# One attention and expert layer on one core: the main scores follow the maximum scores by one pipeline step in place of two

## The chip, the core and the metric

The kernel runs on one core of a Trainium2 chip, as one launch. The core's engines are named here as in the profile: PE is TensorE (matmuls), DVE is VectorE, ACT is ScalarE, POOL is GpSimd, SP is SyncE, which issues most of the DMAs. The metric is the device time of one execution in microseconds, and smaller is better. Before the change three runs gave a median of 390.14 us, from 389.27 to 390.70.

## The reference

The input is x, 32 sequences of 128 rows of 128 numbers, and ctx of the same shape. The layer computes, cut to what matters:

```
q = layernorm(x);  k = v = ctx                       # 16 heads of 8
energy = einsum('nqhd,nkhd->nhqk', q, k)
attn = softmax(energy / sqrt(128));  out = attn @ v
x = x + tanh(g_xattn) * (out @ w_out.T + b_out)
logits = layernorm(x) @ Wg                           # 8 experts
two best experts for each row; weights = softmax of the logits over the two
each row is sent to its two experts: gelu(row @ W1[e] + b1[e]) @ W2[e] + b2[e]
x = x + tanh(g_ffn) * (weighted sum of the two answers)
```

## The kernel before, in words

It has two large parts. The first does attention, the second layer norm, the choice of experts and the scattering of rows into an expert-ordered table in DRAM, one sequence of 128 rows after the other. The second part (71 tiles of 128 gathered rows, each through the two matrices of its expert) starts when the last row is scattered and a table of tiles has been computed from the counts. A last short part adds the two answers of each row and stores the result.

The first part is a software pipeline written out by hand. `pipeline(step)` (line 271) calls `step` once for each t from -2 to 41, so 44 steps, on each engine with that engine's own `step`. A step gets twelve stage names, each of them the sequence that this stage handles in this step, t plus the stage's offset, or None where there is none. The offsets stand in one line (269). In this order:

- n (t+2), x (t+1): statistics of the first layer norm, and the normalised row `xn`.
- a (t): PE transposes `xn` and ctx (lines 622, 623), ACT copies them to `kT` and `qT` (525, 527), and PE computes the first half of the maximum scores (`max_scores(a, 0)`, line 598). These are bf16 scores that serve only to find each row's maximum.
- m (t-1): PE computes the second half of the maximum scores, and DVE reduces both halves to `negmax` (`maximum(0)` and `maximum(1)`, line 779, 1.2 us each).
- b (t-3): PE transposes `negmax` (line 605), ACT copies it to `mT` (510), PE computes the main scores in f32 (630) and subtracts the maxima by a matmul with `pick` (635), and ACT takes the exponential (534). POOL adds the bias to x (442) and copies the values (454).
- p (t-4): probabilities times values (671), and ACT's copy of them (539). q (t-5): transposes and normalisation (652, 813, 820). c (t-6): output projection, x updated, statistics (608, 645, 816, 826). w, r, k (t-7, t-8, t-9): second layer norm, logits, choice, places. d (t-10): POOL scatters the sequence's rows by two indirect DMAs (line 427).

The engines meet at semaphores. Each engine runs its instructions in the order of its step function: on PE the transposes of b, c, r, then those of a, then the main scores of b, then the second half of m's maximum scores, then the small matmuls of c, r, q, k, then 671, and last the first half of a's maximum scores. Both halves of the maximum scores write the same two PSUM banks, so each waits for the reduction of the half before it: `max_scores(s, h)` waits for 2s+h reductions. `negmax` has three buffers, `kT` and `qT` have four, and the main scores' banks wait for the exponentials of the sequence before.

At t = 0 POOL writes its constants, at t = 1 PE transposes the output weights (580, 581) and at t = 2 DVE scales them. PE starts step 2 only when that is done, and POOL's first b waits for it too. SP loads x and ctx in six chunks at the start, and from then on issues one side transfer (expert weights, zeros) for each a.

Of the kernel before, what the change touches and what calls it, by code (L numbers as in the profile page):

```python
# [36 lines left out]
def flamingo_layer(nc, x, ctx, g_xattn, g_ffn, w_out, b_out, Wg, W1, b1, W2, b2, out):  # L37
# [29 lines left out]
    with ExitStack() as es:  # L67
# [198 lines left out]

            return CHUNKS.index(s) if s in CHUNKS[:-1] else None

        N_AT, X_AT, A_AT, M_AT, B_AT, P_AT, Q_AT, C_AT, W_AT, R_AT, K_AT, D_AT = 2, 1, 0, -1, -3, -4, -5, -6, -7, -8, -9, -10

        def pipeline(step):

# [677 lines left out]
```

How the kernel before makes its waits and increments, by code:

```python
        def wait(eng, semaphore, value):  # L248
            if isinstance(value, int) and value < 1:
                return
            eng.wait_ge(semaphore, value)
# [1 line left out]
        def wait_alone(eng, semaphore, value):  # L254
            eng.wait_ge(const_done, 1)
            eng.wait_ge(semaphore, value)
# [23 lines left out]
        def write_pads(eng, experts):  # L282
            eng.wait_ge(pad_tab_done, 1)
            ends = [eng.value_load(pad_tab[0:1, e:e + 1], min_val=0, max_val=PAD_ROW) for e in experts]
            for u in range(NX):
                eng.wait_ge(row_out[u], 32 * (B // NX))
            for r in ends:
                eng.dma_start(xs_dram[bass.ds(r, P), :], pad[:, :]).then_inc(pads_out, 16)
# [22 lines left out]
        @block.sync  # L312
# [30 lines left out]
                pair = slice(k // 2 * 2, k // 2 * 2 + 2)  # L343
                if k < E and k % 2 == 0:
                    sp.dma_start(ex_sb[:, pair, 0:FF], w1v[:, pair, :]).then_inc(moe_loaded, 16)
                elif k < E:
                    sp.dma_start(w2s[:, pair], w2v[:, pair]).then_inc(moe_loaded, 16)
                elif k == E:
                    sp.dma_start(ex_sb[:, :, FF:FF + D], b2.partition_broadcast(P)).then_inc(moe_loaded, 16)
                elif k <= E + NZ:
                    sp.dma_start(zrows[k - E - 1], zeros[:, :]).then_inc(zeroed, 16)
            sp.wait_ge(pool_const, 1)
            def step(t, n, x, a, m, b, p, q, c, w, r, k, d):
                if a is not None and a >= 2:
                    sp.wait_ge(qkT_ready, a)
                    side_transfer(a - 2)
```

## Time and profile before

| what | us |
|---|---|
| median of three runs | 390.14 |
| the profiled execution | 391.28 |
| its span | 389.0 |
| PE, DVE busy in the span | 307.3, 274.0 |
| ACT, POOL busy in the span | 222.6, 223.2 |
| first part, until POOL's last scatter has been issued | 205.17 |
| first matmul of the expert part | 215.27 |

The profile is of one execution. What lies around the span is the difference between 391.28 and 389.0, which is 2.28 us. The steps of the pipeline can be found on PE: from t = 3 to t = 34 a step starts with line 605, once for each sequence of stage b, 32 times. A timeline row gives the start, the length, the engine and line, the operation with its tiles, how many instructions of this kind were run together (x8), and in brackets how long the engine had been idle before it and what released it.

### The profile page before, as it was taken

To read this page: it belongs to the slowest core of one execution; us is meant where nothing else is said; L and a number is where in the kernel's file an instruction comes from. 1 tells how busy PE (TensorE), PEld (TensorE's weight loads), DVE (VectorE), ACT (ScalarE), POOL (GpSimd) and SP (SyncE) were. 2 spreads that over 40 slices of the span, in tenths; PEclk is the share of its full clock that TensorE was granted. 3 is DMA by queue.
4 is the path that set the end of the run, shared out by engine and by line. 5 is a ranking of instruction groups with operands and counts; after the bars stand their busy time and mean duration, and the time that the engine had idled before them with its cause. 6 is when DMAs were issued, how large, how long until landed. Compare 5 with 4: busy or idle time off the path is not lost.

```text
span 389.0 us, 13777 instructions
## 1 busy us (share of the span) xinstructions
PE 307.3 (79%) x3993; PEld 251.1 (65%) x3994; DVE 274.0 (70%) x1084; ACT 222.6 (57%) x656; POOL 223.2 (57%) x367
## 2 busy tenths in 40 slices
PE   1688988989999999987510899999999999999100
PEld 0345665656666566665410899999999998999100
DVE  3858999999999999995673355555555554555296
ACT  2368887777788777765101355555555555555140
POOL 2522457877777877777770155555555555555262
PEclk9999999999999999999955699999999999999655
DMA  7953332122222110100112122222222222221396
GB/s 197 299 168 110 110 98 76 57 79 83 85 78 83 56 52 29 37 31 30 37 48 70 48 69 68 60 63 67 61 64 67 62 64 57 65 61 42 99 358 192
DMA packets 40157, 33.85 MB, mean 87 GB/s; under 512 B 4998, under 2 KB 32936, under 8 KB 40112
## 3 DMA queue, kind: packets, MB, share of 16 engines
q1 hardware_dynamic: 35216, 24.58, 21.6%
q0 software_dynamic: 4320, 8.43, 6.8%
q8 instruction: 25, 0.41, 0.5%
q10 hardware_dynamic: 576, 0.26, 0.3%
q14 instruction: 20, 0.16, 0.2%
HBM read 17.95 MB, written 15.77 MB: 87 GB/s over the span
## 4 chain that ended last, share of the span: by engine, by line
PE 36%; DMA 5%; DVE 4%; POOL 3%; issue 3%; SPq 1%; DVEq 0%; POOLq 0%
PE main_scores L697 17%; PE main_scores L711 17%; POOL expert_rows L427 3%; PE max_scores L688 2%; DVE x_all L920 2%; DVE x_all L924 2%; DMA yc<-choice_rows 1%; DMA choice_rows<-y_s,dest 1%; DMA expert_rows<-pad 1%; DMA expert_rows<-xrow,slot_i 1%; DMA xt<-expert_rows 1%; SPq L289 0%; SPq L390 0%; DVE y_s L901 0%; POOL choice_rows L481 0%
## 5 line engine op out<-in xcount | busy, mean ns | idle before, releaser
L481 POOL DMA_INDIRECT choice_rows<-y_s,dest x71 | 78.8, 1110 | 80.0 <-DVE y_s L901 66.2
L552 ACT ACTIVATE hT<-main_scores,ex_cur 128x128 f32<-128x128 f32 x284 | 81.0, 368 | 68.9 <-PE main_scores L697 68.9
L779 DVE TENSOR_REDUCE negmax<-max_scores 128x8 bf16<-128x1024 f32 x64 | 77.7, 1213 | 6.4 <-PE max_scores L598 6.2
L427 POOL DMA_INDIRECT expert_rows<-xrow,slot_i x64 | 64.8, 1012 | 26.9 <-PE mixed L648 14.1
L711 PE MATMUL main_scores<-w_sb,hT 128*128 x568 | 78.9, 282 | 0.3 <-ACT hT L552 0.3
L697 PE MATMUL main_scores<-xtT,ex_cur 128*128 128x128 f32 x568 | 78.2, 282 | 0.8 <-DVE xtT L893 0.8
L697 PEld LDWEIGHTS main_scores<-xtT,ex_cur 128*128 128x128 f32 x568 | 70.6, 195 | 2.1 <-DVE xtT L893 1.0
L891 DVE COPY ex_cur<-ex_sb 128x644 f32 x71 | 35.2, 496 | 49.7 <-ACT hT L552 25.6
L711 PEld LDWEIGHTS main_scores<-w_sb,hT 128*128 128x128 f32 x568 | 68.9, 191 | 1.6 <-issue 0.5
L534 ACT ACTIVATE probs<-main_scores 128x1024 f32<-128x1024 f32 x64 | 62.0, 1021 | 8.4 <-issue 4.9
L630 PE MATMUL main_scores<-qT,kT 32*128 32x512 f32 x256 | 38.4, 669 | 4.0 <-ACT mT L510 3.9
L527 ACT ACTIVATE qT<-mixed,head_mask 128x128 f32<-128x128 f32 x128 | 37.0, 386 | 0.0
L598 PE MATMUL max_scores<-kT,qT 32*128 32x128 bf16 x512 | 27.5, 226 | 11.8 <-DVE negmax L779 6.5
L671 PE MATMUL mixed<-probs,values 128*32 128x128 f32 x1024 | 35.4, 280 | 0.0
L688 PE MATMUL max_scores<-ident,xt 128*128 128x128 f32 x71 | 20.6, 290 | 16.5 <-DMA xt<-expert_rows 16.5
L598 PEld LDWEIGHTS max_scores<-kT,qT 32*128 32x128 bf16 x512 | 17.5, 97 | 22.8 <-issue 14.9
L458 POOL TENSOR_TENSOR rstd<-ve,neg_half 128x1 f32<-128x1 f32 x32 | 17.9, 560 | 24.6 <-DVE ve L764 24.6
L901 DVE TENSOR_TENSOR y_s<-main_scores,ex_cur 128x128 f32<-128x128 f32 x71 | 20.7, 291 | 15.8 <-PE main_scores L711 13.4
L671 PEld LDWEIGHTS mixed<-probs,values 128*32 128x32 f32 x1024 | 26.6, 111 | 1.6 <-issue 0.9
L465 POOL TENSOR_TENSOR rstd<-ve,neg_half 128x1 f32<-128x1 f32 x32 | 17.7, 553 | 13.7 <-DVE ve L764 13.2
L893 DVE COPY xtT<-max_scores 128x128 f32<-128x128 f32 x71 | 20.1, 284 | 7.4 <-PE max_scores L688 7.4
L635 PEld LDWEIGHTS main_scores<-mT,pick 32*128 32x128 bf16 x512 | 12.1, 96 | 17.7 <-issue 17.7
(132 smaller groups left out, 472.8 us busy)
## 6 DMA issues: line engine op xcount, KB each, us to landing
xt<-expert_rows SPq DMA_DIRECT2D x71, 64.5 KB, 1.8
choice_rows<-zeros SPq DMA_DIRECT2D x16, 256.0 KB, 2.3
yc<-choice_rows SPq DMA_DIRECT2D x16, 256.0 KB, 5.9
ex_sb<-in_L_ffn_W_dram SPq DMA_DIRECT2D x4, 512.0 KB, 4.9
w_sb<-in_L_ffn_W_dram SPq DMA_DIRECT2D x4, 512.0 KB, 4.6
out_dram<-x_all SPq DMA_DIRECT2D x8, 256.0 KB, 4.2
x_all<-in_x_dram SPq DMA_DIRECT2D x5, 384.0 KB, 6.0
ctx_all<-in_ctx_dram SPq DMA_DIRECT2D x5, 384.0 KB, 6.3
```

The source lines that it names most:

```text
L427: nc.gpsimd.indirect_dma_start(xs_dram, bass.IndirectOffsetOnAxis(ap=slot_i[:, d % NX, i:i + 1], axis=0), xrow[:, d % NX, i, :], None).the ...
L481: nc.gpsimd.indirect_dma_start(y_dram, bass.IndirectOffsetOnAxis(ap=dest[:, v, :], axis=0), y_s[:, v, :], None, bounds_check=last_row, oob ...
L527: last = nc.scalar.activation(qT[:, a % KQ, j, :], QK_T[:, 0:P], ACT.Copy, scale=head_mask[:, j:j + 1])
L534: nc.scalar.activation(probs[:, b % 2, 2 * g:2 * g + 2, :].rearrange("p g k -> p (g k)"), E_ALL[:, 1024 * g:1024 * g + 1024], ACT.Exp, sca ...
L552: last = nc.scalar.activation(hT[:, v % 2, c, :], H_BANK[v % 2][:, c * P:c * P + P], ACT.Gelu, bias=ex_cur[:, v, FF + D + c:FF + D + c + 1])
L598: last = nc.tensor.matmul(S_BANK[g % 2][:, j * P:j * P + P], qT_high[strip, s % KQ, j, :], kT_high[strip, s % KQ, :], start=True, stop=True)
L630: nc.tensor.matmul(E_BANK[g], kT[strip, b % KQ, :], qT[strip, b % KQ, :, :].rearrange("p j q -> p (j q)"), start=True, stop=False, skip_gr ...
L671: last = nc.tensor.matmul(O_ALL[32 * g:32 * g + 32, h2 * P:h2 * P + P], values[:, p % 2, h2, j, g, :], probs[:, p % 2, g, head:head + P], ...
L697: last = nc.tensor.matmul(H_BANK[v % 2][:, c * P:c * P + P], ex_cur[:, v, c * P:c * P + P], xtT[:, v % 2, :], start=True, stop=True)
L711: last = nc.tensor.matmul(Y_BANK[v % 2][:, 0:D], hT[:, v % 2, c, :], w2_sb[:, bass.ds(e * (NF * D) + c * D, D)], start=(c == 0), stop=(c = ...
L779: V.tensor_reduce(negmax[:, m % 3, 2 * h:2 * h + 2, 0:J], S_ALL[:, :].rearrange("p (g j k) -> p g j k", g=2, j=J), AX.X, ALU.max, negate=T ...
L891: V.tensor_copy(ex_cur[:, v, :], ex_sb[:, bass.ds(e, 1), :].rearrange("p e f -> p (e f)")).then_inc(ex_ready, 1)
```

## The change

Ten stage offsets move by one. n, x, a and m stay, and b and all behind it come one step sooner. So b takes the sequence whose maxima were reduced in the step directly before, where it took the one of two steps before. The distance between b and each stage behind it stays as it was. The last t is B - D_AT - 1, so the pipeline has 43 steps.

```diff
-        N_AT, X_AT, A_AT, M_AT, B_AT, P_AT, Q_AT, C_AT, W_AT, R_AT, K_AT, D_AT = 2, 1, 0, -1, -3, -4, -5, -6, -7, -8, -9, -10
+        N_AT, X_AT, A_AT, M_AT, B_AT, P_AT, Q_AT, C_AT, W_AT, R_AT, K_AT, D_AT = 2, 1, 0, -1, -2, -3, -4, -5, -6, -7, -8, -9
```

On PE, at the start, the instructions from line 598 of step 1 on stand in a row like this before; the row 598 x16 joins the second half of one step and the first half of the same step's next sequence:

```order
L598 MATMUL max_scores<-kT,qT 128x128 x16
L622 MATMUL mixed<-ident,xn 128x128
L623 MATMUL mixed<-ident,ctx_all 128x128
L598 MATMUL max_scores<-kT,qT 128x128 x16
L605 MATMUL mixed<-ident_b,negmax 128x128
L622 MATMUL mixed<-ident,xn 128x128
L623 MATMUL mixed<-ident,ctx_all 128x128
L630 MATMUL main_scores<-qT,kT 128x512 x4
```

And like this in the changed kernel:

```order
L598 MATMUL max_scores<-kT,qT 128x128 x16
L605 MATMUL mixed<-ident_b,negmax 128x128
L622 MATMUL mixed<-ident,xn 128x128
L623 MATMUL mixed<-ident,ctx_all 128x128
L630 MATMUL main_scores<-qT,kT 128x512 x4
L635 MATMUL main_scores<-mT,pick 128x128 x16
L598 MATMUL max_scores<-kT,qT 128x128 x16
```

The step that held only 622, 623 and 598 (step 2) now holds the transposed maxima and the main scores of the first sequence too.

On PE, near the end of the pipeline, the rows behind the last row 598 (the second half of the last sequence's maximum scores, step 32) are these before, cut at the first row of step 34's kind; line 605 here starts step 33:

```order
L605 MATMUL mixed<-ident_b,negmax 128x128
L608 MATMUL mixed<-ident,attn 128x128
L611 MATMUL mixed<-ident,xrow 128x128
L630 MATMUL main_scores<-qT,kT 128x512 x4
L635 MATMUL main_scores<-mT,pick 128x128 x16
L645 MATMUL mixed<-woutT,aT 128x128
```

In the changed kernel the 31st line 605 is still in a step with maximum scores:

```order
L605 MATMUL mixed<-ident_b,negmax 128x128
L608 MATMUL mixed<-ident,attn 128x128
L611 MATMUL mixed<-ident,xrow 128x128
L630 MATMUL main_scores<-qT,kT 128x512 x4
L635 MATMUL main_scores<-mT,pick 128x128 x16
L598 MATMUL max_scores<-kT,qT 128x128 x8
L645 MATMUL mixed<-woutT,aT 128x128
```

What moved: before, two steps (33 and 34) compute main scores with no maximum scores beside them, and afterwards one step (33) does.

## Rows read from the trace of the kernel before

**Rows 1.** The page: span, busy shares, and TensorE's granted clock in 40 slices.

```profile
span 389.0 us, 13777 instructions
...
PE 307.3 (79%) x3993; PEld 251.1 (65%) x3994; DVE 274.0 (70%) x1084; ACT 222.6 (57%) x656; POOL 223.2 (57%) x367
...
PEclk9999999999999999999955699999999999999655
```

**Rows 2.** Windows view: length, busy time (instructions) of each engine, clock, DMA.

```profile
core 0: us, PE busy (x) PEld busy (x) DVE busy (x) ACT busy (x) POOL busy (x), PEclk, DMA share, GB/s
64.00:159.08 95.08, 87.60 (x1566) 59.10 (x1567) 92.73 (x397) 74.56 (x198) 74.54 (x145) 1.00 0.19 66
169.36:174.39 5.03, 3.96 (x78) 2.86 (x78) 4.74 (x19) 2.91 (x6) 3.59 (x7) 1.00 0.10 30
174.39:179.18 4.79, 3.72 (x69) 2.62 (x70) 2.52 (x19) 2.87 (x6) 3.60 (x7) 1.00 0.10 29
179.18:184.20 5.02, 3.73 (x70) 2.64 (x70) 2.57 (x19) 2.81 (x6) 3.75 (x8) 1.00 0.12 39
```

**Rows 3.** Timeline of PE, fill: start, length, line, operation, [idle before].

```profile
14.09 0.47 PE L622 MATMUL mixed<-ident,xn 128*128 128x128 f32 x1
...
18.05 0.29 PE L605 MATMUL mixed<-ident_b,negmax 128*128 128x128 bf16 x1
...
18.69 2.09 PE L630 MATMUL main_scores<-qT,kT 32*128 32x512 f32 x8
...
21.00 0.64 PE L598 MATMUL max_scores<-kT,qT 32*128 32x128 bf16 x8
...
23.59 0.29 PE L605 MATMUL mixed<-ident_b,negmax 128*128 128x128 bf16 x1
...
27.19 1.88 PE L671 MATMUL mixed<-probs,values 128*32 128x128 f32 x32
29.01 0.40 PE L598 MATMUL max_scores<-kT,qT 32*128 32x128 bf16 x8
29.58 0.23 PE L605 MATMUL mixed<-ident_b,negmax 128*128 128x128 bf16 x1 [0.17 <-ACT oS L539]
...
33.96 0.23 PE L605 MATMUL mixed<-ident_b,negmax 128*128 128x128 bf16 x1 [0.29 <-ACT oS L539]
```

**Rows 4.** Timeline of DVE, fill: the last reduction of step 1, the first of step 2.

```profile
12.07 1.21 DVE L779 TENSOR_REDUCE negmax<-max_scores 128x8 bf16<-128x1024 f32 x1
...
14.07 1.22 DVE L779 TENSOR_REDUCE negmax<-max_scores 128x8 bf16<-128x1024 f32 x1
```

**Rows 5.** Timeline of PE, full steps: first and last start of line 605.

```profile
63.99 0.23 PE L605 MATMUL mixed<-ident_b,negmax 128*128 128x128 bf16 x1
...
164.34 0.23 PE L605 MATMUL mixed<-ident_b,negmax 128*128 128x128 bf16 x1 [0.16 <-ACT oS L539]
```

**Rows 6.** Timeline of PE, drain: the first matmuls of steps 33, 34 and 35.

```profile
174.39 0.23 PE L605 MATMUL mixed<-ident_b,negmax 128*128 128x128 bf16 x1 [0.49 <-ACT oS L539]
...
179.18 0.23 PE L605 MATMUL mixed<-ident_b,negmax 128*128 128x128 bf16 x1 [0.49 <-ACT oS L539]
...
184.20 0.33 PE L608 MATMUL mixed<-ident,attn 128*128 128x128 f32 x1 [0.71 <-ACT oS L539]
```

**Rows 7.** Timeline of POOL, drain: first and last of the last 14 scatters.

```profile
185.47 1.05 POOL L427 DMA_INDIRECT expert_rows<-xrow,slot_i  x1 [0.86 <-PE mixed L611]
...
204.22 0.95 POOL L427 DMA_INDIRECT expert_rows<-xrow,slot_i  x1 [0.30 <-issue]
```

**Rows 8.** Timelines of DVE and PE, one full step: second reduction, and line 605 behind it.

```profile
104.70 1.21 DVE L779 TENSOR_REDUCE negmax<-max_scores 128x8 bf16<-128x1024 f32 x1
...
106.60 0.23 PE L605 MATMUL mixed<-ident_b,negmax 128*128 128x128 bf16 x1
```

**Rows 9.** Windows view, behind the drain: the expert part's first matmuls, and the clock.

```profile
218.00:220.00 2.00, 2.00 (x11) 2.00 (x10) 0.35 (x2) 1.14 (x4) 0.00 (x0) 0.50 0.26 63
220.00:222.00 2.00, 2.00 (x20) 2.00 (x20) 0.50 (x2) 1.14 (x4) 0.00 (x0) 0.99 0.13 33
```

## The prediction, as it was made before the changed kernel ran

> **What bounds the kernel now.** I read the page first, then the busy times of stretches, then the timelines of PE and DVE at both ends of the pipeline. The page [rows 1] says that PE is busy 79% of the span and DVE 70%, which names no bound, because the parts differ. The windows [rows 2] do. In the stretch from 64.0 to 159.08 us, when every stage is at work, DVE is busy 92.73 of 95.08 us (98%), PE 87.60, ACT 74.56, POOL 74.54. So in a full step DVE sets the pace, with PE close behind. Such a step lasts (164.34 - 63.99) / 19 = 5.28 us [rows 5]: the two starts of line 605 are those of steps 12 and 31.
>
> At the ends it is otherwise. In steps 33 and 34, which start at 174.39 and 179.18 [rows 6], DVE is busy only 2.52 of 4.79 and 2.57 of 5.02 us [rows 2]. There the chain PE, ACT, PE, DVE within a step is the bound. In the fill, step 2 (14.09 to 18.05) has only front stages, and steps 3 and 4 (18.05 to 23.59, 23.59 to 29.58) have the main scores too [rows 3].
>
> Both ends lie on the path that sets the end: the expert part waits for the last scatter. POOL issues the last 14 scatters from 185.47 to 204.22 [rows 7], and the tables, the pad rows and the first gather stand behind them.
>
> **The sum.** No instruction is added or taken away in number. What changes is which stages share a step. Call a step's front its n, x, a, m and its back the rest. Before, step t holds front t and the back that begins with sequence t-3; now it begins with t-2. So one step with a front alone goes (old step 2), one step with a back alone goes (old step 33), and the two halves so freed are one more full step. Step by step:
>
> 1. Steps 0 and 1 are the same to the instruction, and end at 14.09 as before.
>
> 2. New step 2 does what old step 3 did: line 605, the transposes, the main scores at 2.09 us for eight, line 635, both halves of the maximum scores and a reduction between them [rows 3]. It needs the maxima of sequence 0. The reduction that ends them runs from 12.07 for 1.21 us [rows 4], so it is over at 13.29, before the step starts. Old step 3 took 23.59 - 18.05 = 5.54 us. New step 2 then ends at 14.09 + 5.54 = 19.63, and new step 3 starts with what old step 4 started with at 23.59. Gain: 3.96 us, exactly old step 2. The first reduction of step 2 (14.07 to 15.29 [rows 4]) lies beside the main scores.
>
> 3. From there new step t does what old step t+1 did, up to the end of the fronts. A step's fronts come later in time than before (front 3 at 19.6 where it was 18.05), so no chunk of x or ctx can be late that wasn't, and SP's side transfers move by the same 1.5 us or so to the later side; the expert weights are not wanted before 215 us.
>
> 4. The fronts end with step 31 in both. So new steps 3 to 31 are old steps 4 to 31 and one full step more: minus 5.28 us.
>
> 5. New step 32 is like old step 32 (5.03 us). Step 33 is like old step 34. Old step 33 is gone: plus 4.79 us.
>
> 6. From old step 35 on (184.20 [rows 6], POOL's scatter at 185.47) everything is as it was, one step number sooner: the same 14 scatters, tables, pads. This tail moves with what is ahead of it.
>
> Sum: 3.96 + 4.79 - 5.28 = 3.47 us less. The profiled execution of 391.28 us (span 389.0 and 2.28 around it) would be 387.81, its span 385.5. It was 1.14 us above the median, so the median becomes 390.14 - 3.47 = 386.67.
>
> **The wait that is made shorter.** Line 605 of sequence s now reads `negmax` that DVE wrote in the step before. By the code this costs nothing at any step: line 605 in step t+1 asks for 2(t-1)+2 = 2t reductions, and the first half of a's maximum scores, the last thing that PE did in step t, has asked for 2t as well. PE never reaches line 605 without them. The trace shows the same distance in a full step [rows 8]: the second reduction ends at 104.70 + 1.21 = 105.91 and line 605 starts at 106.60, 0.69 us later. Queued behind it on PE is the whole step, and ACT's `mT`, so this would be dear if it were wrong. In the fill, 13.29 against 14.09, the slack is 0.8. Below nothing it can't go either, since these waits were no wait before. I take 0; the upper end is the rival below. The buffers get looser: `kT`, `qT` and `negmax` are free one step sooner, and no row shows that anything waits for them, so I take 0 for that too, at most the 2.35 us (95.08 - 92.73) by which DVE is idle in 18 full steps [rows 2], since DVE can't gain more than that.
>
> **The clock.** Step 2's matmuls, and those of steps 3 and 4, run at half speed: eight of line 598 take 0.64 us at 21.00 and 0.40 from 29.01 on [rows 3]. The granted clock in the page [rows 1] reads near full in these slices, so it doesn't show this early stretch; the row lengths do. PE went to full speed between 27.19 and 29.01, that is 8.5 to 10.3 us after the first main scores (18.69), the first dense work. My sum assumes that the rise moves with the work, and so comes near 24.5. The same holds at the start of the expert part, where the granted clock is 0.50 until 220 and 0.99 behind it [rows 9], some 4.7 us after that part's first matmul (215.27 in the table of times). If either rise is half a step off, the half-speed stretch is some 2 us longer or shorter, and half of that is time: 1 us either way.
>
> The Trainium skill, "TensorE: Matmul & The Clock Gate", part 1 (the clock gate), says that the half rate is the default, that sustained activity releases it, and that the point of release differs from run to run, because the watch doesn't start with the kernel. By this rule the rise need not follow the work by the same distance, which would be the second rival below; the rows before show one rise in the fill only, so this trace can neither confirm nor deny it.
>
> **Rivals.**
>
> The forecast, 386.7 us, own range 385.4 to 388.1: chance 0.68.
>
> The clock rises where it did, at some 28.4 us, though the work is earlier. Then new step 3 is slow to its end and takes some 6.4 in place of 5.99 us, so it ends at 26.0, and the 2.4 us that follow are done at half speed: they hold what takes about 2.4 x 4.38 / 6.4 = 1.6 us at full speed (4.38 is old step 5, 29.58 to 33.96 [rows 3]). Loss 0.4 + 0.8 = 1.2 us, so 387.9. For it speaks that 9 us of dense work had to pass before; against it, that the dense work itself begins 4 us sooner. Chance 0.11, half of it beyond the 0.5% line.
>
> It gains more: the earlier dense work, now with main scores directly behind the first maximum scores, raises the clock a step sooner than the shift. Old step 4 (5.99) would be near old step 5 (4.38): 1.6 us more, 385.1. Chance 0.05.
>
> No change: POOL, not the chain, holds the drain. In old step 33 POOL is busy 3.60 of 4.79 us [rows 2]. If POOL were behind there, dropping the step would give back only its idle time, 4.79 - 3.60 = 1.19, and the sum is 3.96 + 1.19 - 5.28 = -0.13: 390.3. For it speaks that the last scatters run one behind the other; against it, that POOL is idle in a quarter of each of the steps before, so it enters the tail with no backlog. Chance 0.08.
>
> Slower: line 605 does wait for the reduction in every full step, so the chain reduction, 605, `mT`, main scores, maximum scores, reduction closes into a ring longer than 5.28 us. It decides as soon as the wait is over 3.47 / 29 = 0.12 us in each of 29 steps. At most it is a reduction less today's distance, 1.21 - 0.69 = 0.52 us; at 0.3 it would cost 29 x 0.3 = 8.7, less 3.5: 395.3. For it: DVE is the bound and the ring goes through it. Against it: the equal counts above. Chance 0.05.
>
> The change does only half of what it says: the fill gains, but the full step that comes back is longer than it looks or the drained steps are not shorter, so that the net is under 1 us: 389.6. Chance 0.03.
>
> **How the numbers follow.** The predicted time is the forecast's, 386.7 us. Its bounds are the clock's 1 us either way and 0.3 us of scatter. Left out of 385.0 to 389.0 are the no-change, slower and half-gain cases (0.16) and a thin tail below, 0.2 in all at most. 0.5% is 1.95 us, about what a measurement can tell here, so faster means below 388.2: 0.66 of the forecast, 0.06 of the clock rival, and 0.05 of the larger gain, together 0.77, and with the share of the half-gain cases that fall there 0.8. Within 0.5%: the rest of the clock case, the POOL case and the half gain, 0.15. Slower 0.05.
>
> **What would show it.** PE's line 605 first at about 14.1 and 19.6 us, 32 times; full steps of 5.28 us; the last matmul of line 598 near 173 us, 1.3 us later than before, but line 605's last start near 175.7 in place of 179.18; POOL's last scatter near 200.8; the first matmul of the expert part near 211.8, and the expert part as long as it was. Wrong for the ring: idle time before line 605 put down to DVE's `negmax`, and full steps over 5.4 us. Wrong for the clock: eight of line 598 at 0.61 us beyond 25 us. Wrong for POOL: the scatters at the usual place, near 204, though PE has finished early.

## The result: 2.2 us faster where 3.5 were forecast

On the chip of the first measurement the kernel before took 390.69 us (median of 20 runs, 389.27 to 392.43) and the changed kernel 388.77 us (20 runs, 387.05 to 389.57). The ratio is 0.9944, with a 95% interval from 0.9932 to 0.9956, so 2.2 us faster, from 1.7 to 2.7 (the two medians lie 1.9 us apart). The forecast was 3.47 us (386.7 us, from 390.14), range 385.0 to 389.0. The time lies in that range and the direction is right. It lies above 385.4 to 388.1, the narrower range of the forecast's own case, and of the 2.1 us between 386.7 and 388.77 some 0.55 are the base, which measured 390.69 in place of 390.14. The gain is 0.6 of what was forecast.

The page of the changed kernel, the lines that answer to [rows 1]:

```profile
span 386.6 us, 13778 instructions
...
PE 307.7 (80%) x3993; PEld 251.2 (65%) x3994; DVE 274.2 (71%) x1084; ACT 222.6 (58%) x656; POOL 222.6 (58%) x367
...
PEclk9999999999999999999655799999999999999655
```

The same work is done in 2.4 us less of span in this pair of traces. The starts of the steps on PE, which answer to [rows 3] and [rows 6], are in its timeline (start, length, engine, line, operation, idle before it):

```profile
13.81 0.29 PE L605 MATMUL mixed<-ident_b,negmax 128*128 128x128 bf16 x1
...
14.50 2.09 PE L630 MATMUL main_scores<-qT,kT 32*128 32x512 f32 x8
...
19.40 0.29 PE L605 MATMUL mixed<-ident_b,negmax 128*128 128x128 bf16 x1
...
23.00 1.22 PE L671 MATMUL mixed<-probs,values 128*32 128x128 f32 x32
...
24.99 0.23 PE L605 MATMUL mixed<-ident_b,negmax 128*128 128x128 bf16 x1
...
170.96 0.23 PE L605 MATMUL mixed<-ident_b,negmax 128*128 128x128 bf16 x1 [0.16 <-ACT oS L539]
...
175.99 0.23 PE L605 MATMUL mixed<-ident_b,negmax 128*128 128x128 bf16 x1 [0.49 <-ACT oS L539]
...
181.00 0.33 PE L608 MATMUL mixed<-ident,attn 128*128 128x128 f32 x1 [0.71 <-ACT oS L539]
...
212.12 0.91 PE L688 MATMUL max_scores<-ident,xt 128*128 128x128 f32 x2 [16.36 <-DMA xt<-expert_rows]
```

The main scores of the first sequence start at 14.50, inside step 2, and steps 2, 3 and 4 start at 13.81, 19.40 and 24.99. No line 605 waits for `negmax`. The 32 matmuls of line 671 at 23.00 take 1.22 us, where those at 27.19 took 1.88 in the kernel before, so PE comes to full speed about 4 us earlier than it did: the rise came with the work. In the drain, step 32 starts at 170.96, step 33 at 175.99, and what was step 35 starts at 181.00 in place of 184.20.

The tail moved as a block: the last 14 scatters on POOL answer to [rows 7].

```profile
182.27 1.05 POOL L427 DMA_INDIRECT expert_rows<-xrow,slot_i  x1 [0.85 <-PE mixed L611]
...
201.04 0.96 POOL L427 DMA_INDIRECT expert_rows<-xrow,slot_i  x1 [0.30 <-issue]
```

From the first of them to the last it is 18.77 us, and 18.75 before. In this pair of traces the pipeline ends 204.22 - 201.04 = 3.18 us sooner, near the 3.47 of the forecast, while the spans differ by 2.4 and the 20 runs say 2.2. So the question is what a typical pair gives, and which term is too large.

**Which term.** The steps from the first full-speed one to the end of the fronts are 27 before (steps 5 to 31) and 28 after (steps 4 to 31). Their length in the windows view, the kernel before first (columns as in [rows 2]):

```profile
29.58:169.36 139.78, 127.64 (x2321) 86.78 (x2322) 134.55 (x544) 110.91 (x293) 98.50 (x199) 1.00 0.22 73
```

And the changed kernel:

```profile
24.99:170.96 145.97, 132.72 (x2408) 90.17 (x2409) 140.39 (x566) 115.23 (x304) 102.45 (x206) 1.00 0.23 74
```

The difference is 6.19 us, not 5.28. Of it 5.84 us are DVE's busy time and 0.35 its idle time, where an average full step [rows 2] has 5.15 busy and 0.13 idle. The full step that comes back is 0.9 us dearer than a mean full step, 0.7 of it in DVE's busy time and 0.2 in its idle time.

### The profile page after: what moved, and what is told of

The parts are those of the page before. It is cut to its first block, busy times and chain, and to the rows that moved or that the text cites. A ratio compares the mean times of both kernels' runs of the same rounds, so it can differ in the third digit from the quotient of the medians.

```text
span 386.6 us, 13778 instructions
## 1 busy us (share of the span) xinstructions
PE 307.7 (80%) x3993; PEld 251.2 (65%) x3994; DVE 274.2 (71%) x1084; ACT 222.6 (58%) x656; POOL 222.6 (58%) x367
## 4 chain that ended last, share of the span: by engine, by line
PE 35%; DMA 6%; DVE 3%; POOL 3%; issue 3%; SPq 1%; DVEq 1%; POOLq 0%
PE main_scores L697 16%; PE main_scores L711 16%; POOL expert_rows L427 3%; PE max_scores L688 2%; DMA choice_rows<-y_s,dest 2%; DVE x_all L920 2%; DVE x_all L924 1%; DMA yc<-choice_rows 1%; DMA expert_rows<-pad 1%; DMA expert_rows<-xrow,slot_i 1%; SPq L390 1%; DMA xt<-expert_rows 0%; DVEq L888 0%; SPq L289 0%; DVE y_s L901 0%
```

## The experiments

Four chips were met. The kernel before takes 390 to 392 us on two of them (that of the first measurement, and that of the last group of experiments below) and 398 us on the two others. Runs are compared only with runs on the same chip.

**The pipeline alone, and second traces.** Both cut kernels leave out the 71 expert tiles (gather, both matmuls, gelu, scatter of the answers), so they don't compute the layer; SP waits for the zeros where it waited for the answers. PE's line stands for the other engines here:

```
-            tiles(pe, early, front, back)
```

cut_before: 

> The kernel before without the 71 expert tiles: the gather, both expert matmuls, gelu and the scatter of answers are left out on all engines, so the last part adds zeros. What is left is the pipeline, its tail of scatters, tables and pads, and the last part. Both theories expect about 390.7 less the expert part, which lasted from 215.3 to some 365 us in the trace: 240 to 246 us. It is the base for the changed kernel cut in the same way.

cut_after: 

> The changed kernel with the same 71 tiles left out. Theory A (the pipeline gains 3.2 to 3.5 us in every run, and the expert part gives back 1.1 to 1.3 us of it): 3.2 to 3.5 us under cut_before. Theory B (the pipeline itself gains only some 2 us in the typical run, and the two profiled runs were an odd pair): 1.9 to 2.3 us under cut_before.

Measured: 242.98 us (242.30 to 243.88) and 238.89 us (238.36 to 239.94), six runs each, so 4.1 us, ratios to the kernel before 0.6113 (0.6090 to 0.6136) and 0.6011 (0.5988 to 0.6034). The kernel before took 398.20 us on this chip. Neither theory had said 4.1 (3.2 to 3.5, and 1.9 to 2.3). Both were made from the first chip, and this is another one.

before_again: 

> The kernel before, unchanged, for a second trace. Theory A: the expert part's first matmul at 215 to 215.6 us, the span from there on 173.3 to 174.2. Theory B: the first matmul 1 us earlier than in the first trace, near 214.2.

after_again: 

> The changed kernel, unchanged, for a second trace. Theory A: first expert matmul at 211.8 to 212.4 us, and 174.2 to 175 us from there to the end of the span, about 0.7 to 1 us more than in the kernel before. Theory B: first expert matmul near 212.1 to 213, and 173.7 us from there on, as before.

Measured: 399.06 and 393.55 us, one run each. The first expert matmul is at 222.19 and 217.45 us, so both traces lie outside what was written, again on the slower chip. From there to the end of the span it is 396.9 - 222.19 = 174.7 before and 391.6 - 217.45 = 174.2 after. That the expert part gives something back was theory A, and it isn't so in this pair. Full steps last 5.43 us on this chip before and 5.41 after (mean of steps 12 to 29), where the first chip has 5.28 and 5.31. DVE is the pace there too (busy 95.4 of 97.8 us in those 18 steps before), so one can look for rows of DVE that are longer. Two are, line 788 and by a little line 793 (mean 382 ns, 339 on the first chip). In the view by lines, from 64 to 160 us, the first chip and then this one (count, busy us, mean ns, idle us):

```profile
L788 DVE TENSOR_TENSOR chosen<-iota,topi 128x16 bf16<-128x16 f32 x18 | 3.0, 166 | 0.0
```

```profile
L788 DVE TENSOR_TENSOR chosen<-iota,topi 128x16 bf16<-128x16 f32 x18 | 5.0, 277 | 0.0
```

The two are 0.11 + 0.04 = 0.15 us more for each step, the whole difference.

**Whole and cut side by side, and the opposite change.** The edit of lag3, against the kernel before (beside it the buffers of `kT` and `qT` go from 4 to 5 and those of `negmax` from 3 to 4, with their indices and waits, so that no new wait comes in):

```diff
-... = 2, 1, 0, -1, -3, -4, -5, -6, -7, -8, -9, -10
+... = 2, 1, 0, -1, -4, -5, -6, -7, -8, -9, -10, -11
```

after_timed: 

> The changed kernel, unchanged, timed beside the cut pair on one chip. Theory A (a part of the pipeline's gain is given back in the expert part, on every chip): it gains 1 us less than the cut pair shows on the same chip. Theory C (the expert part is as long in both, and what differs is how much the pipeline gains from chip to chip and from run to run): the same gain as the cut pair within 0.6 us.

cut_before_2: 

> The kernel before without the 71 expert tiles, as in cut_before, once more, as the base on this chip. All theories: 241 to 244 us if the chip is the one of cut_before, some 4 us less if it is like that of the first trace.

cut_after_2: 

> The changed kernel without the 71 expert tiles. Theory A: 3.2 to 4.1 us under cut_before_2. Theory C: under cut_before_2 by what after_timed is under the kernel before, within 0.6 us.

lag3: 

> The same change in the other direction: the main scores three steps behind the maximum scores, so 45 steps, with five buffers of kT and qT and four of negmax so that no wait is new. The theory of the sum (a front-only step and a back-only step against a full one) expects one more front-only step of 3.9 to 4.0 us at half clock or 3.1 to 3.5 at full clock, one more back-only step of 4.8 to 5.2 and one full step of 5.3 to 5.4 less: 3.0 to 3.9 us slower than the kernel before. The rival (the number of steps is not what counts, the shorter distance is) expects no more than 1 us.

Measured: the changed kernel 393.32 us against 398.01, ratio 0.9885 (0.9855 to 0.9916), so 4.6 us; the cut pair 244.47 and 239.98 (ratios 0.6151, 0.6128 to 0.6174, and 0.6029, 0.6007 to 0.6052), so 4.5 us. The whole gains what the cut pair gains within 0.2 us, as theory C said. Theory A asked for 1 us less. The whole's interval is wide, 3.3 to 5.8 us, so these runs alone don't shut it out; together with the traces they speak against it. lag3 is 402.55 us, ratio 1.0110 (1.0075 to 1.0145), so 4.4 us slower, a little over its 3.0 to 3.9, which lie within its interval of 3.0 to 5.8. The rival's 1 us does not. In its trace the last part of the drain starts at 192.58 us, and at 188.62 in cut_before_2 on the same chip, so 4.0 us later. A step of distance costs in one direction what it gives in the other, as it should if what counts is how many steps hold a front or a back alone.

**The clock, the fill alone, and the last pair.** The warm kernels add this on PE ahead of the expert part, to the kernel before and to the changed one:

```diff
+            for i in range(115):
+                nc.tensor.transpose(M1[:, 0:P], ident[:, :], ident[:, :])
```

fill_only adds a rest of the back stages to the changed kernel at t = 16, so that they follow at the new distance ahead of it and at the old one behind it. The heart of its edit:

```diff
+            if stage < M_AT:
+                if t == PAUSE:
+                    return None
+                t -= t > PAUSE
```

warm_before: 

> The kernel before with 115 more transposes of the identity on PE between the pipeline and the expert part, where PE is idle for 16 us; nobody reads their result. The theory that the clock's rise is part of the spread: granted clock 1.0 at the expert part's first matmul, so its first matmuls take 1.06 us for eight in place of 1.9 to 2.1; 1.8 to 2.2 us faster than the kernel before, and the stretch from the first expert matmul to the end of the span near 172.3 us. Rival (something else limits the expert part's start): under 0.5 us.

warm_after: 

> The changed kernel with the same 115 transposes. If what the pipeline gains reaches the end in full once the clock is out of play, it is 3.2 to 3.8 us faster than warm_before on a chip like the first, 4 to 4.7 us on the chip of the second and third calls. If 1 us is given back in the expert part by anything but the clock, it is 1 us less than that. As a version of its own: 1.8 to 2.2 us faster than the changed kernel.

fill_only: 

> The changed kernel whose back stages rest for one step in the middle (t = 16) and then follow two steps behind as before, so 44 steps. The fill is that of the changed kernel, the drain that of the kernel before, and a front-only step lies in the middle at full clock. The sum says: old step 2 (4.0 us) saved, a front-only step at full clock paid. DVE's work for a front is 2 x 1.21 + 0.34 + 0.28 + 0.18 + 0.15 = 3.4 us, less overlap some 3.1, and POOL's and ACT's chains make it at most 4.0: 0 to 0.9 us faster than the kernel before. Rival (all of the gain is in the fill): as fast as the changed kernel.

after_third: 

> The changed kernel, unchanged, to compare the three others on the same chip. On a chip where the kernel before takes 390 to 391 us: 1.9 to 3.5 us under it. On one where it takes 398 us: 4.0 to 4.7 us under it.

The kernel before took 391.68 us here (24 runs), and after_third 388.91 us, ratio 0.9934 (0.9910 to 0.9958), so 2.6 us faster, inside what was written.

warm_before was 391.83 us, ratio 1.0004 (0.9987 to 1.0022): nothing gained, which lies within the rival's bound of 0.5 us. Its PE timeline says why:

```profile
198.96 15.24 PE L681 MATMUL mixed<-ident 128*128 128x128 f32 x115 [0.74 <-DVE carry L833]
215.67 0.30 PE L691 MATMUL max_scores<-ident,xt 128*128 128x128 f32 x1 [1.47 <-DMA xt<-expert_rows]
...
216.41 1.10 PE L700 MATMUL main_scores<-xtT,ex_cur 128*128 128x128 f32 x8
217.35 0.27 PE L691 MATMUL max_scores<-ident,xt 128*128 128x128 f32 x1
217.50 1.89 PE L700 MATMUL main_scores<-xtT,ex_cur 128*128 128x128 f32 x8
```

The first eight matmuls of line 700 take 1.10 us, at full speed as wanted. The next eight take 1.89, at half: between the end of the transposes (214.20) and there PE had waited 1.47 us and less, and the clock fell all the same. The half-speed stretch was moved, not removed. So this says nothing of what the clock would give. warm_after was 388.56 us, ratio 0.9922 (0.9892 to 0.9951), so not 1.8 to 2.2 but 0.3 us under the changed kernel on this chip, for the same reason: the windows of its trace show the granted clock at 0.65 from 213 to 215 us and at 0.50 from 215 to 217. Against warm_before it is 3.3 us faster by the medians, inside the 3.2 to 3.8 that were written; with intervals of some 1 us on either ratio that doesn't tell it from 2.6.

The pair shows the terms without the odd half-speed step of the first trace. Steps 3, 5 and 32 of warm_before on PE:

```profile
17.68 0.29 PE L605 MATMUL mixed<-ident_b,negmax 128*128 128x128 bf16 x1
...
28.81 0.23 PE L605 MATMUL mixed<-ident_b,negmax 128*128 128x128 bf16 x1 [0.18 <-ACT oS L539]
...
168.62 0.23 PE L605 MATMUL mixed<-ident_b,negmax 128*128 128x128 bf16 x1 [0.15 <-ACT oS L539]
```

And steps 2, 4 and 32 of warm_after:

```profile
13.64 0.29 PE L605 MATMUL mixed<-ident_b,negmax 128*128 128x128 bf16 x1
...
24.82 0.23 PE L605 MATMUL mixed<-ident_b,negmax 128*128 128x128 bf16 x1 [0.25 <-ACT oS L539]
...
170.81 0.23 PE L605 MATMUL mixed<-ident_b,negmax 128*128 128x128 bf16 x1 [0.16 <-ACT oS L539]
```

Step 4 of warm_after starts at 24.82, so its 28 steps take 145.99 us, against 139.81 us for the 27 of warm_before. That is 6.18 us for one step, the same as in the first pair.

The cut pair on the 398 us chip differs. Step 5 and step 32 of cut_before:

```profile
28.15 0.23 PE L572 MATMUL mixed<-ident_b,negmax 128*128 128x128 bf16 x1 [0.17 <-ACT oS L514]
...
171.22 0.23 PE L572 MATMUL mixed<-ident_b,negmax 128*128 128x128 bf16 x1 [0.54 <-ACT oS L514]
```

Steps 4 and 32 of cut_after:

```profile
24.57 0.23 PE L572 MATMUL mixed<-ident_b,negmax 128*128 128x128 bf16 x1 [0.17 <-ACT oS L514]
...
172.95 0.23 PE L572 MATMUL mixed<-ident_b,negmax 128*128 128x128 bf16 x1 [0.53 <-ACT oS L514]
```

Here it is 148.38 - 143.07 = 5.31 us, a little below this chip's mean step, and 5.33 in each of the two other pairs of traces on such chips. So the dear step belongs to the 390 us chips.

fill_only was 393.72 us, ratio 1.0058 (1.0036 to 1.0080): 2.3 us slower, from 1.4 to 3.1, where 0 to 0.9 faster was written, and both theories of it fell. The fill did as it should: step 3 starts at 19.41, as in the changed kernel. What was wrong is the price of the front-only step in the middle. PE's timeline at steps 16 and 17:

```profile
86.46 0.30 PE L632 MATMUL mixed<-ident,xn 128*128 128x128 f32 x1 [0.74 <-DVE carry L840]
86.59 0.27 PE L633 MATMUL mixed<-ident,ctx_all 128*128 128x128 f32 x1
88.07 0.41 PE L608 MATMUL max_scores<-kT,qT 32*128 32x128 bf16 x8 [1.20 <-DVE negmax L789]
90.13 0.40 PE L608 MATMUL max_scores<-kT,qT 32*128 32x128 bf16 x8 [1.65 <-DVE negmax L789]
90.47 0.23 PE L615 MATMUL mixed<-ident_b,negmax 128*128 128x128 bf16 x1
...
91.62 2.09 PE L640 MATMUL main_scores<-qT,kT 32*128 32x512 f32 x8 [0.15 <-ACT mT L520]
```

The step in which PE waits twice for a reduction ends at 90.47, and then eight main-score matmuls take 2.09 us where 1.14 is usual: the granted clock is 1.00 until 90.47 and 0.50 from 92 to 94 us. The thin step let the clock fall to half, and the next full step pays for it. Steps 15 to 17 take 9.98 + 6.32 us in place of two full ones (10.5), so the front-only step costs 5.8 us with its consequence; over the whole stretch from step 4 to step 32, against steps 5 to 32 of warm_before, it is 5.3, since step 18 is 0.2 us shorter and the stretched steps 15 and 19 of that kernel are not there. The fill gives 3.9 in this pair, and so the last scatter comes 1.4 us later (204.93 against 203.50). The profiled run is the fastest of the twelve (391.90 us); why the median is 1.8 us above it isn't shown.

## Why the prediction was right in sign and too large in size

**Steps 0 to 2, the fill (3.96 us): right.** Step 3 of warm_before and step 2 of warm_after start at 17.68 and 13.64, so 4.04 us apart; in the first pair it is 18.05 - 13.81 = 4.24, of which 0.28 is that step 2 starts at 13.81 in place of 14.09. New step 2 lasts 5.59 us, and 5.54 was taken.

**No new wait at line 605: right.** No trace has idle time there that is put down to `negmax`. (On the 398 us chips PE is idle ahead of it for 0.4 to 0.5 us in most full steps of both kernels, put down to ACT's `oS` or DVE's `carry`.) Between the end of the fill and the end of the fronts only the dear step is left to explain.

**The full step that comes back (5.28 us): this is the term that was mis-sized.** It is 6.19 and 6.18 us on the 390 us chips and 5.31 to 5.33 on the others. I took a mean over 19 steps, but steps differ: most last 5.26 us, and some are stretched. Before they are steps 11, 15 and 19 (5.72, 5.58, 5.61); after they are steps 10, 21, 22, 26 and 30 (5.71, 5.48, 5.71, 5.57, 5.60). They stand in the same steps in both traces of the old pipeline and in all three of the new on such chips, so they are no noise. (Steps 11 before and 10 after are equally long and cancel.) In all of them but step 21 DVE pauses with no releaser in the profile. Of the changed kernel, in step 22, DVE's timeline:

```profile
118.91 0.09 DVE L784 MATCH_VALUE_LOAD topi<-top_all,lg 128x8 f32 x1 [0.26 <-issue]
118.99 0.16 DVE L784 FIND_INDEX8 topi<-top_all,lg 128x8 uint32<-128x8 f32 x1
119.07 1.20 DVE L779 TENSOR_REDUCE negmax<-max_scores 128x8 bf16<-128x1024 f32 x1
120.19 0.17 DVE L788 TENSOR_TENSOR chosen<-iota,topi 128x16 bf16<-128x16 f32 x1
120.27 0.54 DVE L793 TENSOR_SCALAR xn<-x_all,mv,rstd 128x128 f32<-128x128 f32 x1
...
125.62 0.34 DVE L793 TENSOR_SCALAR xn<-x_all,mv,rstd 128x128 f32<-128x128 f32 x1
```

DVE stands still for 0.26 us ahead of line 784, and in the same step line 793 takes 0.54 us, where it takes 0.34 a step later. These are two different things, and together they are the 0.9 us.

The pauses come at 55.21, 118.91, 140.06 and 160.97 us in the changed kernel and at 59.03, 80.73 and 101.93 in the kernel before. Counted over all of DVE's records in the trace, semaphore waits with them, they stand ahead of records 192, 575, 703 and 831, and 191, 319 and 447, so 128 records apart or three times that, give or take one. From 0.66 to 0.71 us after the end of each, the DMA records have one packet of 8 KB of the kind that they call instruction, as here in step 15 of the kernel before, from 79.76 to 85.34 us (queue and kind, packets, MB, share of the engines):

```profile
q14 instruction: 1, 0.01, 0.5%
```

DVE's records are as many in both kernels, but in another order, so the same counts fall on other instructions, and at the multiples of 128 that are missing here no pause over 0.2 us shows. That DVE waits there for its next instructions is what this suggests, and no run tried it. The four pauses are 1.03 us and the three 0.80, which is the 0.2 us of idle time.

The 0.7 us of busy time are three rows in the changed kernel: line 793 at 56.44 and 120.27 (0.2 us too long each) and line 788 in step 21 (0.31 too long). The other long rows of these two lines are in both kernels. POOL's scatter stands beside the last of the three:

```profile
56.44 0.54 DVE L793 TENSOR_SCALAR xn<-x_all,mv,rstd 128x128 f32<-128x128 f32 x1
...
114.27 0.48 DVE L788 TENSOR_TENSOR chosen<-iota,topi 128x16 bf16<-128x16 f32 x1
```

```profile
113.91 1.05 POOL L427 DMA_INDIRECT expert_rows<-xrow,slot_i  x1 [0.58 <-issue]
```

Line 788 starts 0.36 us after the scatter's start and ends 0.83 after it. Usually it starts 0.67 after it and takes 0.17, and so ends at the same point. In the fourteen traces, 144 of the 145 rows of line 788 that take over 0.175 us between 30 and 175 us end 0.83 to 0.85 us after the start of POOL's scatter, however long they are. So this row is held until that point, while one that starts 0.18 to 0.31 us after the scatter takes its usual 0.17; what holds it isn't shown. Line 793 is long where it starts 0.02 to 0.03 us after POOL's line 442, in place of 0.33 ahead of it. On the 398 us chips line 788 is held in nearly every full step. POOL's scatter is later there: it waits a mean of 0.43 us with no releaser in before_again and 0.26 in the first trace. There it is in both kernels alike, and that fits a step that comes back at 5.3 us.

**The drain (4.79 us): right.** Steps 32 and 33 last 5.03 and 5.01 us after, as steps 32 and 34 did (5.03 and 5.02), and the old step 33 of 4.79 is gone.

**The sum with the measured terms.** 4.04 + 4.80 - 6.18 = 2.66 us, and the last scatter of the warm pair moves by 203.50 - 200.87 = 2.63. The two comparisons of the whole kernels on such chips gave 2.2 and 2.6 us. The first pair's 3.18 has 0.4 more because step 4 before was at half speed to its end (5.99 us; 5.59 in warm_before). That this trace came so near to 3.47 was luck: one error hid the other.

**The clock: right as a bound.** The rise went with the work. It isn't at a fixed distance: steps 3 and 4 before lasted 5.54 and 5.99 us in the first trace, 5.54 and 5.59 in warm_before, 4.99 and 5.39 in cut_before. That is a spread of 1.15 us over the two steps, and new steps 2 and 3 spread as much (5.58 and 6.03 in after_again, 5.04 and 5.39 in cut_after), about what the term of 1 us either way was meant to hold. The Trainium skill, "TensorE: Matmul & The Clock Gate", part 1, says that the point of release differs from run to run, and these lengths agree. The rival in which the clock rises at 28.4 us though the work is earlier, for 1.2 us, is in no trace.

**The rivals.** POOL holding the drain is refuted, since the scatters moved with PE. The ring through line 605 is refuted. The expert part gives nothing back as a rule: from its first matmul to the end of the span it lasts 173.8, 174.7 and 175.1 us in three traces of the old pipeline, and 174.5, 174.2, 174.4, 174.0 and 174.1 in five of the new. In the first pair by itself it did, 0.7 us, which is why the spans differ by 2.4 and not 3.2. There the stretch at half speed at its start is some 1 us longer after the change. Before, the clock is back at about 220.0 [rows 9], 4.8 us after the first matmul; in the changed kernel's windows it is back at about 217.9, 5.8 us after the first matmul, by this row:

```profile
217.00:219.00 2.00, 2.00 (x16) 2.00 (x16) 0.29 (x1) 1.12 (x4) 0.00 (x0) 0.77 0.14 33
```

**What stays open.** On the 398 us chips the gain is 4.1 to 4.6 us. In the three pairs of traces there the fill gives 3.6, 3.9 and 3.8 us (with the two steps behind it), the drain 5.2 each time, and the full step takes 5.3, so that the drain's last part starts 3.5, 3.8 and 3.7 us sooner. What comes behind does not go with the change: from there to the last scatter it takes 22.0, 21.3 and 22.0 us in three traces of the kernel before (whole or cut) and 21.3, 21.3, 22.0 and 22.0 in four of the changed one. The longer time goes with a granted clock that falls some 2 us into this part, as in before_again, where the part starts at 188.44:

```profile
189.00:191.00 2.00, 1.63 (x37) 1.62 (x40) 0.73 (x5) 0.39 (x2) 1.05 (x1) 0.96 0.02 4
191.00:193.00 2.00, 0.65 (x13) 0.19 (x4) 1.54 (x14) 0.30 (x1) 1.68 (x3) 0.50 0.21 70
```

The shorter goes with a fall after 7 to 8 us, as in after_again, where it starts at 184.75:

```profile
191.00:193.00 2.00, 0.68 (x8) 0.36 (x6) 1.53 (x12) 0.36 (x2) 1.69 (x3) 0.87 0.14 41
```

So 3.5 to 3.8 of the 4.1 to 4.6 us are accounted for, and the rest is not. Why POOL's scatter is later on these chips wasn't settled either, nor what DVE's pauses are.

## What to carry to other kernels

When a software pipeline loses a step, write down which stages shared the steps that go and which full step comes back: here a front-only step of 4.0 us and a back-only step of 4.8 to 5.2 against one full step of 5.3 to 6.2. The mean over a long stretch doesn't price the step that comes back to better than 1 us here, even with its stretched steps counted in, since a new order shifts where the pauses fall and which rows of two engines meet. And before a thin step is put into the middle of a dense pipeline, count what the clock does behind it.

## What the runs showed that was not expected

- One thin step of about 5 us, in which PE waited 0.74, 1.20 and 1.65 us, was enough to bring the granted clock from 1.00 to 0.50 in the next step: 2.09 us for eight matmuls where 1.14 is usual.
- 115 matmuls back to back kept the clock up only until pauses of 1.47 us and less came behind them: 1.10 us for eight matmuls, then 1.89.
- The same kernel takes 390 to 392 us on some chips and 398 on others, 0.15 us of it in each full step, and the same change gains 2.2 to 2.6 us on the one kind and 4.6 on the other.
- A small DVE row beside POOL's scatter ends 0.83 to 0.85 us after the scatter's start, whether it starts 0.36 or 0.67 us after it: 0.48 us for a row that usually takes 0.17.
- DVE pauses of 0.21 to 0.31 us stand a multiple of 128 records apart, each followed by one 8 KB packet of the kind instruction.
